# A four-layer decoder on one core: projections moved between the first products of each attention, and, for heads of width 8, the row maxima carried by a ninth row of the queries

## What is computed

```python
scores = jnp.einsum('btghk,bThk->bghtT', qg, k)
scores = jnp.where(mask, scores, -jnp.inf) / np.float32(np.sqrt(K))
p = jax.nn.softmax(scores, axis=-1)
out = jnp.einsum('bghtT,bThv->btghv', p, v)
```

## Time and profile before

| | us |
|---|---|
| median of 3 runs | 2002.5 (2000.7 to 2007.37) |
| profiled execution, its own time | 1997.6 |
| its span | 1995.8 |
| TensorE matmul busy | 1566.4 (78%) |
| VectorE busy | 1134.8 (57%) |
| ScalarE busy | 610.3 (31%) |
| mean granted TensorE clock | 0.862 of full |

### The profile page before, as it was taken

One profiled execution on the slowest core, in us unless ns is written; L12 is line 12 of the kernel. 1 busy time (PEld: TensorE's weight loads), 2 busy tenths in 40 slices (PEclk: granted clock), 3 DMA queues, 4 the chain that ended last, 5 costly groups with the idle time before them and its releaser, 6 DMA issues. The chain is left out here.

```text
span 1995.8 us, 23570 instructions
## 1 busy us (share of the span) xinstructions
PE 1566.4 (78%) x8740; PEld 718.1 (36%) x8740; DVE 1134.8 (57%) x2827; ACT 610.3 (31%) x839; POOL 131.8 (7%) x156
## 2 busy tenths in 40 slices
PE   1798659994666888885978997985988479994984
PEld 0332334441233433444433323352436223343342
DVE  5685544446966666644455854545454556744445
ACT  1265332223314023321432651411221124541331
POOL 1000000001000500000000000000000103321000
PEclk9799769996978999996997997886986778997687
DMA  4000000003000000000010000000010000000000
GB/s 187 0 2 1 1 1 0 0 0 124 0 1 1 21 22 2 1 1 1 0 75 18 1 1 0 1 1 1 0 63 0 1 0 1 1 1 1 1 1 11
DMA packets 4081, 27.37 MB, mean 14 GB/s; under 512 B 384, under 2 KB 2432, under 8 KB 2944
## 3 DMA queue, kind: packets, MB, share of 16 engines
q1 hardware_dynamic: 2912, 25.35, 3.2%
q10 hardware_dynamic: 1056, 0.52, 0.1%
HBM read 25.34 MB, written 0.52 MB: 13 GB/s over the span
## 5 line engine op out<-in xcount | busy, mean ns | idle before, releaser
L704 ACT ACTIVATE big<-banks 128x1024 f32<-128x1024 f32 (+2 forms) x320 | 294.2, 958 | 427.8 <-PE banks L507 260.2
L602 DVE TENSOR_REDUCE maxima<-banks 128x1 f32<-128x512 f32 (+4 forms) x640 | 362.5, 603 | 100.9 <-PE banks L476 94.2
L503 PE MATMUL banks<-big 32*128 32x512 f32 (+6 forms) x1280 | 259.5, 656 | 16.8 <-DVE negmaxT L615 16.4
L476 PE MATMUL banks<-big 32*128 32x77 bf16 (+6 forms) x1024 | 161.2, 306 | 30.3 <-DVE maxima L602 18.3
L537 PE MATMUL banks<-big,v_heads 128*9 128x512 f32 (+7 forms) x1024 | 164.3, 585 | 5.8 <-ACT heads_out L657 2.9
L342 POOL TENSOR_TENSOR rstd<-mean_var,minus_half 128x4 f32<-128x4 f32 x46 | 46.9, 1020 | 1645.8 <-DVE mean_var L317 1645.8
L1110 DVE TENSOR_TENSOR big<-big,banks 128x512 f32<-128x512 f32 (+1 forms) x88 | 60.5, 687 | 130.5 <-PE banks L1058 125.2
L1085 ACT ACTIVATE big<-banks 128x512 f32<-128x512 f32 (+1 forms) x120 | 71.7, 597 | 200.6 <-PE banks L1055 200.6
L1068 PE MATMUL banks<-big,moe_weights 128*128 128x512 f32 (+1 forms) x240 | 123.0, 593 | 2.8 <-DVE big L1107 1.5
L476 PEld LDWEIGHTS banks<-big 32*128 32x128 bf16 (+1 forms) x1024 | 58.0, 100 | 166.3 <-DVE maxima L602 102.9
L503 PEld LDWEIGHTS banks<-big 32*128 32x128 f32 (+3 forms) x1280 | 77.9, 187 | 79.6 <-ACT big L704 36.2
(11 more groups left out here) (368 smaller groups left out, 2246.1 us busy)
## 6 DMA issues: line engine op xcount, KB each, us to landing
moe_weights<-in_moe SPq DMA_DIRECT2D x1, 4896.0 KB, 22.1
moe_weights<-in_moe SPq DMA_DIRECT2D x1, 4864.0 KB, 15.0
moe_weights<-in_moe SPq DMA_DIRECT2D x1, 3264.0 KB, 10.6
moe_weights<-in_l3x SPq DMA_DIRECT2D x1, 3072.0 KB, 10.2
late_weights<-in_l2x SPq DMA_DIRECT2D x1, 2048.0 KB, 8.1
moe_weights<-in_l SPq DMA_DIRECT2D x1, 1234.0 KB, 13.2
rows<-in_rows SPq DMA_DIRECT2D x1, 1152.0 KB, 8.1
late_weights<-in_turned SPq DMA_DIRECT2D x1, 1152.0 KB, 17.3
```

The source lines that it names most:

```text
L476: last = nc.tensor.matmul(RING[n % NR][:, x * klen:x * klen + last_key(t)], q[rows, t * P:(t + 1) * P], ks[rows, 0:last_key(t)], start=Tru ...
L503: nc.tensor.matmul(SC[pair % 2][0:size, j % 2, n0:S], ks[rows, i * P:i * P + size], q[rows, n0:S], start=True, stop=False)
L602: nc.vector.tensor_reduce(dst, src, AX_X, ALU.max).then_inc(ring_free.up(), 1)
L704: nc.scalar.activation(E[pair % NEP][0:size, :, n0:S], SC[pair % 2][0:size, :, n0:S], ACT.Exp, scale=scale).then_inc(exp_ready.up(), 1)
```

## The change

1. **`row_attention` takes `projections` and `needs`.** Queries, keys and values are no longer made in a block of their own. TensorE makes them inside the attention's block, into banks 2 to 5 by turns, between the first products: at first as many as the first group needs, then one before every two units, the remainder in a row behind the last unit. `needs` says how many must be emptied before a group's first products. Scores of round 0 wait until all are emptied. ScalarE empties all of them. Biases of values become a further product of a row of ones with the bias row. All eight attentions do this. In layer 1's causal one only the values move; the rotated queries and keys stay in their block.
2. **Width 8** (four attentions): `negmax` writes minus the maximum in fp32 to the ninth column of each head's 32 in `c.RW` (which GpSimd zeroes at the block's start), TensorE turns it with four fp32 transposes, and VectorE adds the turned bank to the group's queries. The keys' padded places hold 1 in their ninth row. The four bf16 products of line 507 and the copy to `NMT` are left out, and `score_ready` is raised by the second and the fourth score product.
3. **Causal mask** (one attention): in the round before a new group, `soon` comes behind `turn_negmax` on TensorE, and behind `move_negmax` on VectorE.

```diff
+    def project_bank(n):
+        _, rows, cols = projections[n][:3]
+        return c.bank[2 + n % 4][0:rows, 0:cols]
+
+    def project(pe, n):
+        products, _, _, _, after = projections[n]
+        if n >= 4:
+            pe.wait_ge(project_free.sem, project_free.at(n - 3))
+        if after is not None:
+            pe.wait_ge(project_free.sem, project_free.at(after + 1))
+        for m, (lhsT, rhs) in enumerate(products):
+            last = nc.tensor.matmul(project_bank(n), lhsT, rhs, start=(m == 0), stop=(m == len(products) - 1))
+        last.then_inc(projected.up(), 1)
...
     def raw_scores(pe, u):
         (b, k), (j, tl) = groups[u // U], units[u % U]
+        if needs and u % U == 0:
+            pe.wait_ge(project_free.sem, project_free.at(needs[b, k]))
...
-        to = RING[n % NR][:, 0:S // 2].bitcast(BF16)
+        to = RING[n % NR] if turned else RING[n % NR][:, 0:S // 2].bitcast(BF16)
         for t in range(ST):
-            last = nc.tensor.transpose(to[:, t * P:(t + 1) * P], c.NM[:, g % 2, t, :], c.ident_bf[:])
+            negmax_tile, unit = (c.RW[:, g % 2, t, :], c.ident) if turned else (c.NM[:, g % 2, t, :], c.ident_bf)
+            last = nc.tensor.transpose(to[:, t * P:(t + 1) * P], negmax_tile, unit[:])
...
-            nc.tensor.matmul(SC[pair % 2][0:size, j % 2, n0:S], ks[rows, i * P:i * P + size], q[rows, n0:S], start=True, stop=False)
-        for j in range(HB):
+            last = nc.tensor.matmul(SC[pair % 2][0:size, j % 2, n0:S], ks[rows, i * P:i * P + size], q[rows, n0:S], start=True, stop=turned)
+            if turned and j % 2:
+                last.then_inc(score_ready.up(), 1)
+        for j in range(0 if turned else HB):
...
+        if turned:
+            row = c.RW[:, g % 2].rearrange("p t (j w) -> p t j w", j=HB)[:, :, :, 8]
+            if g == 0:
+                dve.wait_ge(room_cleared.sem, room_cleared.at(1))
+            nc.vector.tensor_scalar(row, m, -1.0, None, ALU.mult).then_inc(negmax_ready.up(), 1)
+            return
...
+        if turned:
+            q = queries(*groups[g])
+            nc.vector.tensor_tensor(q, q, RING[n % NR][:, :], ALU.add).then_inc(ring_free.up(), 1)
+            return
...
-            for u in range(min(U + per_round, NU)):
-                raw_scores(pe, u)
+            made, first = 0, 0
+            while first < U + per_round or made < len(projections):
+                wanted = needs[groups[first // U]] if needs and first < U + per_round else 0
+                upto = min(max(wanted, made + (first > 0)), len(projections))
+                for n in range(made, upto):
+                    project(pe, n)
+                made = upto
+                for u in range(first, min(first + 2, U + per_round)):
+                    raw_scores(pe, u)
+                first += 2
             turn_negmax(pe, 0)
+            if projections:
+                pe.wait_ge(project_free.sem, project_free.at(len(projections)))
...
-                for u in soon:
-                    raw_scores(pe, u)
+                turn_first = mask == "causal" and next_group(r) is not None
+                if not turn_first:
+                    for u in soon:
+                        raw_scores(pe, u)
                 if 0 <= r - 1 < R:
                     values(pe, r - 1)
                 if next_group(r) is not None:
                     turn_negmax(pe, next_group(r))
+                if turn_first:
+                    for u in soon:
+                        raw_scores(pe, u)
...
         def _(act):
+            for n, (_, _, _, empty, _) in enumerate(projections):
+                act.wait_ge(projected.sem, projected.at(n + 1))
+                empty(act, project_bank(n)).then_inc(project_free.up(), 1)
```

Layer 2's self attention as one of the eight callers; its two `matmul_stream` blocks are gone:

```diff
+    for half in range(2):
+        for k in range(4):
+            projections.append(tiles_of(c, c.m("L2_WK"), c.XT, K, k, half, bias=bk[:, k:k + 1]))
+            w = c.headmat[:, k * P:(k + 1) * P]
+            d = Q[:, k, half * S:(half + 1) * S]
+            projections.append(([(w, qf[:, 0, half * S:(half + 1) * S])], P, S, act_copy(c, d), half))
+            needs[half, k] = len(projections)
+        projections += [natural(c, c.XT[:, t * P:(t + 1) * P], c.m("L2_WV"), V[:, t, :, 0:8], 8, row=bv)
+                        for t in range(half * ST, (half + 1) * ST)]
+    attention_8(c, [P] * ST, 0.25, projections=projections, needs=needs)
```

More of the change, by code:

```diff
@@ L392, in _, with row_attention @@
                     nc.vector.tensor_copy(dst[:, k, t * P:(t + 4) * P], c.bank[u % 8][:, :]).then_inc(dve_freed.up(), 1)
-def row_attention(c, key_tiles, dk, queries, keys, vop, scale, Y, mask=None):
+def row_attention(c, key_tiles, dk, queries, keys, vop, scale, Y, mask=None, projections=(), needs=None):
     nc = c.nc
@@ L838, in _, with tiles_of, context_tile, natural @@
                 nc.vector.tensor_tensor(dst, dst, bias.unsqueeze(1).broadcast_to([P, NT, P]), ALU.add)
+def tiles_of(c, w, src, dst, k, half, bias=None, after=None):
+    d = dst[:, k, half * S:(half + 1) * S]
+    return ([(w[:, k * P:(k + 1) * P], src[:, half * S:(half + 1) * S])], P, S, act_copy(c, d, bias=bias), after)
+def context_tile(c, w, src, dst, k, bias=None):
+    return ([(w[:, k * P:(k + 1) * P], src)], P, B * SK, act_copy(c, dst[:, k], bias=bias), None)
+def natural(c, srcT, w, dst, width, row=None):
+    n = srcT.shape[1]
+    products = [(srcT, w)] + ([] if row is None else [(c.ones[0:1, 0:n], row[0:1])])
+    return (products, n, w.shape[1], lambda act, bank: c.nc.scalar.copy(dst, bank.rearrange("p (h d) -> p h d", d=width)), None)
 def heads_8(c, klen):
@@ L865, in keys @@
         return K[:, k, b * klen:(b + 1) * klen]
[L867 removed]
+    row_attention(c, key_tiles, 8, lambda b, k: Q[:, k, b * S:(b + 1) * S], keys, vop, scale, c.Y8, projections=projections, needs=needs)
 def block_product(c, aT, bT, dst):
@@ L1018, in cross_attention_8 @@
 def cross_attention_8(c, wq, wk, wv, wo, bq, bk, bv, bo):
-    units, one = cross_kv(c, wk, wv, bk, bv)
-    Q, _ = heads_8(c, SK)
-    for k in range(4):
-        bias = None if bq is None else bq[:, k:k + 1]
-        units += halves(c, lambda half, k=k: [(wq[:, k * P:(k + 1) * P], c.XT[:, half * S:(half + 1) * S])], P, Q[:, k], bias=bias)
-    fill(c, one, 1.0)
-    matmul_stream(c, units)
-    attention_8(c, [SK], 8.0 ** -0.5)
+    ctxT = c.m("ctxT")[0:CTX]
+    Q, K = heads_8(c, SK)
+    v = c.VH[0:SK, 0:B * HEADS * 9].rearrange("p (b h e) -> p b h e", b=B, e=9)
+    fill(c, v[:, :, :, 8], 1.0)
+    col = lambda bias, k: None if bias is None else bias[:, k:k + 1]
+    projections = []
+    for k in range(4):
+        projections += [context_tile(c, wk, ctxT, K, k, bias=c.ninth[:] if bk is None else col(bk, k)), tiles_of(c, wq, c.XT, Q, k, 0, bias=col(bq, k))]
+    projections += [natural(c, ctxT[:, b * SK:(b + 1) * SK], wv, v[:, b, :, 0:8], 8, row=bv) for b in range(B)]
+    projections += [tiles_of(c, wq, c.XT, Q, k, 1, bias=col(bq, k)) for k in range(4)]
+    needs = {(0, k): 2 * k + 2 for k in range(4)} | {(1, k): 11 + k for k in range(4)}
+    attention_8(c, [SK], 8.0 ** -0.5, projections=projections, needs=needs)
     turn(c, c.Y8, NT, P, c.yT8)
@@ L1405, in layer1_ffn @@
     row_attention(c, [P] * ST, 64, lambda b, k: y[:, k, b * S:(b + 1) * S], lambda b, k: K[:, k % 2, b * S:(b + 1) * S],
-                  lambda b, h, i: V[:, b * ST + i, h % 4, 0:64], 0.125, y, mask="causal")
+                  lambda b, h, i: V[:, b * ST + i, h % 4, 0:64], 0.125, y, mask="causal",
+                  projections=[natural(c, nT[:, t * P:(t + 1) * P], c.m("wv"), V[:, t], 64) for t in range(NT)])
     yT = y
```

121 lines of the change are left out of this document (51 added, 70 removed).

## The result

| | before | after |
|---|---|---|
| median of 4 runs each, us | 2002.61 (2000.7 to 2007.37) | 1945.78 (1944.13 to 1946.76) |
| profiled execution, us | 1997.6 | 1946.76 |
| its span | 1995.8 | 1945.0 |
| mean granted TensorE clock | 0.862 | 0.873 |

The ratio is 0.9712 (95% interval 0.9694 to 0.9730): 56.8 us less by the medians, 50.8 by the two profiled executions, where the sum of the prediction said 76.6. Executions in which the chip was in its slower state (one of the kernel with pick in the one-tile attentions, 2719.29 us, and two of the kernel before) are left out of every median here.

The account below looks back on a forecast made before the run. TensorE, busy 78%, was taken to bind unevenly: stalled openings, a low clock, and a loop through ScalarE's exponentials at width 8. Terms 32.3 + 20.5 + 18.2 - 1.4 + 7.0 = 76.6 us gave 1925.9, range 1900 to 1962.

Parts of the forecast that it names:

- Openings: From an attention's first projection to its first scores: projections fill gaps between first products, gain 32.3 us over eight attentions.
- cold part: Extra time as openings start at low clock, kept unchanged in the forecast; 1.8 us in layer 0 self, 2.2 in layer 2.
- Rival 4: Slower: stops for ScalarE's copies keep the clock down while projections run, 46 us more there; about 2032 us; chance 0.03.
- The test given for it: Whether the granted clock is still 0.5 ten microseconds into the openings of layers 2 and 3.
- First rounds: Rounds just after the openings: products between the maxima keep TensorE's clock up, gain 20.5 us.
- Rival 2: The clock falls all the same in first rounds, their gain shrinking from 20.5 to 4 us; total 1942; chance 0.15.
- Width 8, four tiles: Steady groups: products with pick leave the loop over the exponentials, 13.33 to 12.0 us per group, gain 18.2.
- Rival 1: The loop stays in rounds of width 8, or turn and add eat the gain; 18.2 becomes -2, total 1946; chance 0.12.
- The sign predicted for it: In width-8 four-tile rounds, ScalarE's first exponential starts before the second pair's scores.
- Width 8, one tile: Steady cross-attention groups: four products go, the fp32 turn costs more; +0.1 us per group, 1.4 lost over two attentions.
- Causal order: Causal attention: turn ahead of the next group's first products saves 0.47 us at each of 15 groups, 7.0; bounds 0 and 18.
- Table load: ScalarE's load of the exponentials' table, 1.28 us, three times, now behind the last copy while scores run; priced at 0.

Follow-up runs that it names:

- order and lead: Against the changed kernel, single-tile projections go query, key, query tile of one k, values before the last k, three more projections ahead of each group's first products; 1922.39 us.
- The values last: Against the changed kernel, layer 2 self attention's eight value projections come behind all others, emptied by VectorE, which adds the bias; 1942.67 us.
- the run with the lead of three: Against the changed kernel, three more projections are made ahead of each group's first products in the single-tile attentions; 1933.98 us.

## Why the prediction was right, and where it was wrong

- **Verdict and range.** Faster, 20 us above the forecast of 1925.9 and inside 1900 to 1962. The openings alone missed by 32.2; that first rounds gave 7.7 more than forecast and unedited parts 2.8 brought the total nearer, and that is luck.
- **Openings, 32.3 forecast, 0.1 measured.** This is the step that failed. "After the change that cold part falls on whatever comes first, so I keep it" took the cold part as fixed. In the single-tile openings it was 6 to 11 us and became 14 to 21. Single-tile openings lost 12.2 where 8.9 were to be gained, and order and lead, which the forecast kernel did not have, give it all back (75.6, against 79.7 forecast). In layer 2's self attention, the back part (13 projections behind the last first product) took 13.6, not 9.1: a value tile with its bias costs 0.83, not the 0.45 assumed, since the one-row product takes as long as the main one (0.49 and 0.48 for a pair), and the clock fell. The values last gave 27.1, below the 29.3. Self openings of layers 0 and 3 came to 23.8 and 31.3, within 2 us. The causal one gained 0.5 for 3.1, its products all at 0.50.
- **Rival 4 named part of the mechanism, at the wrong price.** It named the stops as what might keep the clock down while projections run. The clock did stay down in four openings, but without the stops two of the four still rose only after 17.6 and 19.8 us: the order was the other part. And the first rounds did not suffer with them: they depend on what stands last. Against the forecast those openings lost 21 us, where the rival had 46 for all openings and 40 for the first rounds. The test given for it, 0.50 ten microseconds into the openings of layers 2 and 3, was met in the single-tile ones.
  The Trainium skill (TensorE: Matmul & The Clock Gate, The HAM clock gate) has activity release the half rate soon after it begins, and everything after it at full rate. In the run with the lead of three TensorE was busy for 19.82 of 20.70 us and stayed at half rate for 17.6, so the measurement goes against that. The doubled times of the products (2.07 against 1.02 us a pair) say the same as the clock record.
- **First rounds, 20.5 forecast.** About 28: layer 3 second 14.1 (forecast 6), layer 2 cross 8.2 (5), cross ones of width 8 about 1.1 each (1.0), layer 3 first 2.4 (2.5), layer 2 self 1.3 (3.5), layer 0 none (1.5). In layer 3's second, five groups at full clock take 18.05, not the "22 to 25", and "gaps of its own" took off still more of the gain. Rival 2 fell as a whole, though what it said of layer 0's last units came true there: the first rounds stayed at 0.68, below the 0.7 that the prediction had set as a sign of being wrong, while the others show 0.76 to 1.00.
- **Width 8, four tiles, 18.2 forecast.** 0.97 per group and 15.8 in all. Rival 1 fell: with the products with `pick` back, groups are 13.32 again. The limit was near VectorE as said, busy 45.25 of 49.40 us, its waits for first products down from 6.7 to 2.5. The loop is not gone everywhere: weight loads of scores waited for an exponential 8 times (4.8 us) in these four groups before, and wait 4 times (2.4) now. The sign predicted for it was wrong: the first exponential still starts only when the second pair's scores are nearly done, since TensorE issues all eight products within 0.7 us. Timeline of the profile after:

```profile
128.33 1.25 PE L527 MATMUL banks<-big 32*128 32x512 f32 x8
129.50 1.02 ACT L758 ACTIVATE big<-banks 128x1024 f32<-128x1024 f32 x1 [1.13 <-PE banks L527]
```

- **Width 8, one tile, 1.4 loss forecast.** 0.31 per group and 3.1 in steady groups. The products and the turn cost what was said: the four products freed 0.21, and the fp32 turn takes 0.50 where the bf16 one took 0.23. Not in this term was that scores stand behind the add of 0.69 us: in one steady group it ends at 243.09, scores start at 243.25, and the seven first products ahead of them take 0.52 instead of 0.25.
- **Causal order, 7.0 forecast.** 7.1 (0.53 per group), by the mechanism named.
- **Table load at 0.** It starts as the last copy ends (at 1611.90, 1.28 us) and the first exponential of layer 3 waits for TensorE until 1613.47. The further drain of the Trainium skill (ScalarE: Activation LUTs, What ACT_TABLE_LOAD costs) shows nowhere in that gap: 0.29 us were left.

## What to carry to other kernels

Work that is moved to fill waits is paid at the clock that its neighbours leave: in these runs it paid, both together by 25 us in four openings, to keep the query tiles (512 columns, 128 rows) together around each short key tile, to give each copy a lead of three products so that TensorE does not stop for it, and to let the stretch end on projections, which kept the next stage's start at full clock. When an edit's own stretch and the total disagree, compare stretch by stretch: a few us at this scale come and go with the clock in parts that were not touched. A product that contracts one row took as long as one that contracts 128 (same columns).

## What was not expected of the hardware

- The same order of products, with TensorE busy throughout, rose to 1.00 after 4.6 us in one attention and after 17.6 or 20.3 in another, and which one it was changed with the lead. It also moved where no edit touched the opening: in five kernels with the same projections layer 1's cross opening rose after 13.6 to 21.8 us. What decides stays open: the moment at which an opening starts was not varied by itself, and each opening was seen in one execution of each kernel.
- A cold start into thin rounds lasts: before the change 30.62 us at 0.51 with TensorE busy 29.81 of them, while the same rounds entered at 1.00 stay there for 18 us.
- In layer 2's opening the clock fell to 0.50 with 6.59 of 6.80 us busy, behind value products of 128 columns and narrow first products (the row of the kernel without bias products; with them 6.00 of 6.00 us at 0.59). With the values moved to the end it did not fall.
